# A state-space kernel's part across chunks as (C times B) times the values, with four moves around it

## The reference

```python
CHUNK = 128
Y_diag = jnp.einsum('bcln,bcsn,bhcls,bcshp->bclhp', Cc, Bc, Lm, Xc)
decay_states = jnp.exp(a_cs[..., -1:] - a_cs)
states = jnp.einsum('bcln,bhcl,bclhp->bchpn', Bc, decay_states, Xc)
...
prev_states = jnp.einsum('bhzc,bchpn->bzhpn', decay_chunk, states)[:, :-1]
Y_off = jnp.einsum('bcln,bchpn,bhcl->bclhp', Cc, prev_states, jnp.exp(a_cs))
return (Y_diag + Y_off).reshape(b, l, h, p)
...
Y = Y + D[None, None, :, None] * xs
y = y * jax.nn.silu(z)
y = y * jax.lax.rsqrt(jnp.mean(y * y, -1, keepdims=True) + 1e-05) * norm_w
out = y @ out_proj_w.T
```

## Time and profile before

| what | value |
|---|---|
| median of 3 runs | 925.86 us |
| the profiled execution's own time | 926.9 us |
| its span, first to last instruction | 925.2 us |
| granted TensorE clock, mean of the span | 0.996 |
| TensorE busy | 904.3 us (98%) |
| TensorE's weight loads | 806.5 us (87%) |
| VectorE busy | 633.4 us (68%) |
| ScalarE busy | 528.6 us (57%) |
| GpSimd busy | 503.8 us (54%) |
| end of the first stage (last scatter issued) | 539.8 us |
| `from_state` (L1650), 32 records | 17.3 us busy |
| `chunk_state` (L1633), 32 records | 16.4 us busy |
| skip products (L588), 32 | 40.5 us busy, mean 1286 ns |

### The profile page before, as it was taken

The page is one execution under the profiler, slowest core; times in us unless marked ns, Lnnn a source line. Parts: engine busy times, 40 slices in busy tenths (PEclk is TensorE's granted clock), DMA queues, the critical chain, the costliest instruction groups (busy, mean ns, idle before and its releaser), DMA issues. The chain is left out here.

```text
span 925.2 us, 17776 instructions
## 1 busy us (share of the span) xinstructions
PE 904.3 (98%) x5832; PEld 806.5 (87%) x5832; DVE 633.4 (68%) x1698; ACT 528.6 (57%) x1097; POOL 503.8 (54%) x498
## 2 busy tenths in 40 slices
PE   8999999999999999999999979999999999999998
PEld 7888798888888888888888779999999999999997
DVE  1587889888988898889889644646464646464633
ACT  1767776677667766776667434444443434343533
POOL 5656877887778777876775522223232323232343
PEclk9999999999999999999999989999999999999999
DMA  7940011001000000000000044343434342523221
GB/s 211 321 154 17 30 47 34 23 34 34 13 23 14 24 13 23 14 25 12 12 14 5 25 138 122 70 109 74 108 70 112 67 115 63 119 58 79 23 58 46
DMA packets 49398, 59.13 MB, mean 64 GB/s; under 512 B 6304, under 2 KB 44683, under 8 KB 49360
## 3 DMA queue, kind: packets, MB, share of 16 engines
q1 hardware_dynamic: 35920, 42.14, 14.1%
q0 software_dynamic: 13440, 16.50, 10.7%
HBM read 33.62 MB, written 30.67 MB: 69 GB/s over the span
## 5 line engine op out<-in xcount | busy, mean ns | idle before, releaser
L690 POOL DMA_INDIRECT out<-ye,tok_slot x56 | 96.0, 1713 | 250.0 <-DMA out<-ye,tok_slot 128.0
L973 ACT ACTIVATE hf<-bank 128x512 f32<-128x512 f32 x128 | 79.3, 620 | 187.1 <-PE bank L1814 187.0
L1423 DVE TENSOR_TENSOR h_lo<-hf,h_hi 128x512 fp32r<-128x512 f32 x128 | 88.8, 694 | 101.5 <-ACT h_hi L975 100.1
L1812 PE MATMUL bank<-w_hi,h_hi 128*128 128x256 f32 x512 | 146.1, 285 | 0.0
L1813 PE MATMUL bank<-w_lo,h_hi 128*128 128x256 f32 x512 | 144.9, 283 | 0.0
L1814 PE MATMUL bank<-w_hi,h_lo 128*128 128x256 f32 x512 | 144.9, 283 | 0.0
L1122 DVE SCALAR_TENSOR_TENSOR xc<-bank,cw,xc 128x253 f32<-128x253 f32 (+2 forms) x288 | 128.2, 469 | 1.9 <-ACT xc L799 0.4
L1812 PE MATMUL bank<-xe_hi,w_hi 128*128 128x512 f32 x256 | 100.0, 391 | 0.0
L1813 PE MATMUL bank<-xe_lo,w_hi 128*128 128x512 f32 x256 | 99.8, 390 | 0.0
L1814 PE MATMUL bank<-xe_hi,w_lo 128*128 128x512 f32 x256 | 99.7, 389 | 0.0
L1813 PEld LDWEIGHTS bank<-w_lo,h_hi 128*128 128x128 f32 x512 | 98.3, 192 | 0.0
(11 more groups left out here) (223 smaller groups left out, 2352.3 us busy)
## 6 DMA issues: line engine op xcount, KB each, us to landing
w_raw<-w SPq DMA_DIRECT2D x16, 1024.0 KB
slots_dram<-zero_row SPq DMA_DIRECT2D x1, 8320.0 KB, 29.9
xe<-slots_dram SPq DMA_DIRECT2D x15, 520.0 KB, 4.5
out<-hb SPq DMA_DIRECT2D x16, 256.0 KB, 2.1
w_raw<-in_wT SPq DMA_DIRECT2D x2, 644.0 KB, 6.2
out<-zero_row SPq DMA_DIRECT2D x1, 1024.0 KB, 32.1
slots_dram<-rows,slot POOLq DMA_INDIRECT x64
out<-ye,tok_slot POOLq DMA_INDIRECT x64
```

What stands on the lines that cost most here:

```text
L690: g.indirect_dma_start(out, bass.IndirectOffsetOnAxis(ap=tok_slot[q][:, j:j + 1], axis=0), ye[q][:, j, :], None, compute_op=ALU.add).then_ ...
L973: sc.activation(hf[m % 2][:, :], h_bank[i % H_BANKS][:, :], ACT.Gelu_apprx_tanh)\
L1423: vc.tensor_tensor(h_lo[:, m, :], hf[m % 2][:, :], h_hi[:, m, :].bitcast(F32), ALU.subtract)\
L1812: te.matmul(out_, hi, rhi, start=first_, stop=False)
```

## The change

The kernel after makes `across`, C of chunk 1 times B of chunk 0 (128x128), in the place of the transposed B, copies it as the other was copied, and multiplies it with `xdec` straight away (`across_chunks`), which gives the part across chunks. `chunk_state`, the copy `state` and `from_state` are gone. On VectorE `carried_y` stands ahead of `first_y` and reads the other bank. On TensorE the dt projection stands ahead of the first `to_yT`. GpSimd waits for the second decay product before the skip products. In the last two half turns a root moves behind `xdec`, and the row descriptions of the last batch go to VectorE. In front of the second stage three filler matmuls stand where six stood.

```diff
@@ gpsimd, half, no front @@
                     if b:
                         decayed_x(b, q)
+                        gated_root(t, p)
+                        pool.wait_ge(m_ready[KD - 1][q], m_ready[KD - 1].now(b, q))
                         skip_x(b, q, 0)
                         skip_x(b, q, 1)
...
                         second_root(b, q)
-                    describe_rows(t, p)
+                        describe_rows(t, p)
                     scatter_rows(t, p)
@@ gpsimd, half, with a front @@
                 if b:
+                    pool.wait_ge(m_ready[KD - 1][q], m_ready[KD - 1].now(b, q))
                     skip_x(b, q, 0)
                     skip_x(b, q, 1)
...
                 if not nf:
                     segment_inputs(f, p, 0)
-                    gated_root(b, q)
                     free_rows(t, p)
@@ scalar @@
-                sc.activation(bs[p][:, :], bank[p][3][:, 0:NS], ACT.Copy)
+                sc.activation(across[p][:, :], bank[p][3][:, 0:P], ACT.Copy)
...
-            def state(r, p):
-                act.wait_ge(state_psum[p], state_psum.now(r, p))
-                copy(st[p][:, :], bank[p][3][:, :], st_ready[p])
@@ vector @@
-                    carried_y.last = back.mark(vc.tensor_tensor(heads(y[p][:, 1, :]), heads(bank[p][2][:, :]),
+                    carried_y.last = back.mark(vc.tensor_tensor(heads(y[p][:, 1, :]), heads(bank[p][3][:, :]),
...
+                def describe_rows(t, p):
+
+                    dve.wait_ge(tok_next[1 - p], tok_next.now(t, 1 - p))
+                    dve.wait_ge(ohs_ready[p], ohs_ready.now(t, p))
+                    vc.tensor_copy(rows[p][:, :, C_TOK].bitcast(I32), tok_iota[:, :])
+                    vc.tensor_copy(rows[p][:, :, C_E0], topf[p][:, :, 0])
+                    vc.tensor_tensor(rows[p][:, :, C_W0:C_W0 + 2], top[p][:, :, 0:2],
+                                     bc(linv[p][:, :].unsqueeze(2), [P, KD, 2]), ALU.mult).then_inc(row_info[p], 1)
...
                 if b:
+                    carried_y(b, q)
                     first_y(b, q)
-                    carried_y(b, q)
...
+                if not f:
+                    describe_rows(t, p)
                 if t:
                     slots_of(t, p)
@@ tensor @@
-                    te.transpose(bank[where][3][:, 0:P], xc[p][:, KI, 0:P], ident[:, :])
+                    te.matmul(bank[where][3][:, 0:P], xc[p][:, KI, 0:P], xc[p][:, KI + 1, P:2 * P], start=True, stop=True)
...
-                def chunk_state(r, p):
+                def across_chunks(r, p):
 
                     pe.wait_ge(decay_ready[p], decay_ready.now(r, p, 2))
                     pe.wait_ge(bs_ready[p], bs_ready.now(r, p))
                     pe.wait_ge(xdec_ready[p], xdec_ready.now(r, p))
-                    te.matmul(bank[p][3][:, :], bs[p][:, :], xdec[p][:, :], start=True, stop=True)\
-                        .then_inc(state_psum[p], 1)
+                    te.matmul(bank[p][3][:, :], across[p][:, :], xdec[p][:, :], start=True, stop=True)\
+                        .then_inc(yo_psum[p], 1)
...
-                def from_state(r, p):
-                    pe.wait_ge(st_ready[p], st_ready.now(r, p))
-                    pe.wait_ge(decay_ready[p], decay_ready.now(r, p))
-                    te.matmul(bank[p][2][:, :], xc[p][:, KI + 1, P:2 * P], st[p][:, :], start=True, stop=True)\
-                        .then_inc(yo_psum[p], 1)
...
-                    keep_clock(0, 6)
+                    keep_clock(0, 3)
```

23 lines of the change are left out of this document (8 added, 15 removed).

## The result

The kernel after takes 930.01 us (median of 6 runs, 928.97 to 932.84), the kernel before 926.24 in the same series: a ratio of 1.0049, 95% interval 1.0031 to 1.0067. The forecast was 920.8 us. The change costs 4 us where I had expected it to give 5. The profiled execution has a span of 928.3 us against 925.2, so +3.1 us, at a mean granted clock of 0.992 against 0.996.

A forecast was written before the change was run, and what follows sets the result against it. VectorE's loop with ScalarE was taken to set 30.88 us a half turn, TensorE adding 0.16; 0.74 + 2.1 + 0.5 + 1.1 + 0.4 plus a guessed 0.2 gave 5.0 us off 925.86: 920.8 us, range 912.3 to 924.5.

The forecast's parts named there:

- the paragraph on the merged product: TensorE, path across chunks: 0.74 us less work per batch; 0.74 us gained in the first full half turn, 2.1 us after.
- The gain of 13 x 0.16 us: Steady half turns: TensorE adds 31.04 - 30.88 = 0.16 us to VectorE's loop; removing it gives 2.1 us, bounds 0 and 9.6.
- the first kind: Steady half turns where `lmax` waits 0.51 us for TensorE's router product; in the other kind VectorE has no sizable TensorE wait.
- The skip products: GpSimd, moved behind the second decay product: contention only passes to another operation, zero in steady part; bounds -0.8 and +0.1 us.
- TensorE's 0.74 us: First full half turn: `nmax` waits 1.62 us for TensorE, so the merged product's net saving of 0.74 us is gained whole.
- The drain and the scatters: Last batch: decay products freer of skips, 0.5 us gained; last row descriptions on VectorE, 1.1 us gained.
- The guess of 0.2 us: Between the last `nmax` and the drain: 0.2 us added for waits on TensorE.
- The three fillers: Joint to the second stage: three filler matmuls fewer start the first product sooner, gain 0.4 us; bounds +0.8 and -1.2.
- (a): Rival: TensorE is the bound after all, so 15 x 0.74 = 11.1 us come through; 912.6 us, chance 0.13.
- (b): Rival: VectorE slips out of a collision with GpSimd, its loop losing 0.8 to 1.1 us; 916.9 us, chance 0.14.
- (c): Rival: GpSimd wakes late, skip products start late and `oh` stands behind one; slower, 932.4 us, chance 0.08.
- (d): Rival: the steady part gives nothing and the fillers cost 1.2 us; 925.5 us, chance 0.10.

The follow-up runs named there:

- e3: Kernel before with only the dt projection moved ahead of the transposes of the first gated rows; 926.47 us, ratio 1.0000.
- e7: Kernel before with GpSimd's bias addition moved behind the second chunk's gated root; 925.21 us, ratio 0.9988.
- e4: Kernel after without GpSimd's wait for the second decay product in the looped half turns; 932.91 us, ratio 1.0064.
- e1: Kernel after plus one useless fp32 128x512 TensorE product where the removed product from the state stood; 928.03 us, ratio 1.0021.
- e11: Kernel before with bias addition late, GpSimd's two coefficients reported one by one, and statistics ahead of the first decay product; 934.53 us, ratio 1.0097.
- e15: Kernel after plus a whole useless product (fp32, 512 columns) ahead of the transposes of the hidden rows, in the wait; 933.83 us, ratio 1.0078.
- e6: Kernel after with GpSimd's bias addition moved behind the second chunk's gated root; 929.56 us, ratio 1.0039.
- e18: Kernel after with the merged product moved behind the transposes of the hidden rows; 933.57 us, ratio 1.0075.
- e19: Kernel after with bias addition late, coefficients reported one by one, 24 fillers for 38, merged product behind the hidden rows' transposes; 931.69 us, ratio 1.0067.

## Why the prediction was wrong

**The step that failed** is the end of the paragraph on the merged product: TensorE "would then idle for 0.3 us more in each, and I expect the wait for `hn` in every one". Both halves came true in kind (the wait is there in nine of the ten undisturbed turns, and idle time rose by 0.63 us, from 0.26 to 0.89), and I had costed them at nothing. They came with three falls of the granted clock to 0.50, at 2.1 us each, 6.4 us in the profiled run. The runs of one and the same kernel say the same: the kernel after takes 928.97 us at a clock of 0.994 and 932.84 at 0.988. The clock had been looked at only at the joint, never as a price of slack.

What is shown: the falls come with the missing product (e3 and e7 have none, e4 has three), each costs what the window says, and a whole useless product in the place of the old one ends them (e1), with all other moves of the change left in. What isn't shown is what decides. Idle time is not the measure: e11 idles 0.52 us a turn without a fall, e15 only 0.33 with four. The Trainium skill, page "TensorE: Matmul & The Clock Gate", section "A second HAM failure mode: psum-queue depth-cycling", tells of a kernel in which TensorE paused briefly but often between groups of matmuls and swung between its two clock levels. The trace here agrees in kind: the clock fell to 0.50 and came back, and the only pauses of TensorE in the half turn of the fall at 179 us are 0.27 and 0.15 us long. The page gives no rule that would tell e11 from e15. What decides stays open.

**The gain of 13 x 0.16 us** didn't come either. I had put the 0.16 us down to TensorE, and e4 contradicts that: with TensorE relieved and GpSimd's queue as before, `lmax` still waits for it in every other turn, and turns of the first kind stay, at 31.15 and 31.24 us. What ended the first kind is TensorE's relief together with GpSimd's wait, and the same two moves made the second kind longer, 31.00 us on average where e4 has 30.90. The skip products were booked at zero in the steady part, and the sum was right about there, but as an exchange: the collision with the second decay product is gone (1.23 to 1.25 us in every turn), and `topf` and `oh` meet a skip product in every turn. The two kinds differ not only in the wait of `lmax`, as I had it, but in which operation meets the skip product: the decay product and `oh` take 2.01 and 0.19 us in the first kind, 1.25 and 0.99 in the second. The base was thin as well: 30.88 us was read from one turn, and the seven turns of the second kind before average 30.98 (one takes 31.45). "Contention goes from one operation to the next" stood in the text for `oh`; the rule of two SBUF inputs that went with it takes in too little, since `lv` and `topf` read one operand each and are held up as well.

**The ends.** In the first full half turn, where all of TensorE's 0.74 us was to come through, 0.28 us came (30.34 to 30.06 us); that the row of the table shows 0.72 is luck. A new wait of 0.38 us stands ahead of the dt projection there (54.22 us), half of the relief. The drain and the scatters were right, 1.70 of 1.6 (decay products 3.25 us together, scatters 1.28 us apart). The guess of 0.2 us between the last `nmax` and the drain was 0.99. **The three fillers** gave 0.06 us of loss instead of 0.4 of gain: TensorE arrived there 1.6 us later, from the 38 fillers ahead, so that their number no longer set the first product.

**Rivals.** (a) is refuted: TensorE's busy time in an undisturbed turn fell from 30.78 to 30.16 us, by 0.62 and not 0.74, and the turns did not get shorter. (b) didn't occur by itself; forced, in e6, it shows that the collision's 1.1 us are no gain: TensorE's products and another collision take them up at once. (c) didn't occur: the skips start at 269.37, 0.08 us behind the end of the second decay product, and `oh` stays at 0.99. (d) had the sign of the end right and not the mechanism. None held a clock that falls in the steady part, and that is why the range ended at 924.5.

## What to carry over

Slack on TensorE can have a price of its own: where it is 99% busy at the full clock, look at the granted clock turn by turn after every matmul that is taken out, and in several runs. When the loops of several engines lie within one or two per cent of each other, as they seem to here, a saving on one of them can be worth nothing (31.04 and 31.05 us). A wait that goes away has to be tested against each move of the change by itself before it is put down to one of them. A piece of the span that starts at zero has the scatter of the start in it. A useless product that is to keep the clock has to be tried in its place: the same one ended the falls in one place and left four of them in another.

## What the hardware showed unexpectedly

In the kernels that keep the order of the kernel after, falls start at one place of the turn (behind the start of the narrow dt projection), in e18 and e19 ahead of it, at the transposes of `hn` or the narrow products beside them, and never in every turn: in the profiled run of the kernel after at 179, 306 and 432 us, 126 us or four turns apart; in e15 at 149, 245, 340 and 436, 96 us or three turns apart. These rows don't show what sets the spacing.

VectorE operations of a few elements can be held up for a whole microsecond beside a GpSimd operation: a 128x2 `lv` takes 0.16 us free and 1.27 us beside the bias addition, and when the addition was moved away (e6) a 128x1024 product some 5 us later took 2.01 us instead of 1.23, beside a GpSimd operation that now came later.
